# Last attention of a hybrid model: four exponentials per visit to the values, eight probability buffers, two buffers of masked keys, selections over 128 rows

## The reference

```
qkv = x @ W_qkv.T + b_qkv
scores = jnp.einsum('bqhd,bkhd->bhqk', Q, K)
scores = jnp.where(causal, scores, -jnp.inf)
probs = jax.nn.softmax(scores / sqrt(hd), axis=-1)
out = jnp.einsum('bkhd,bhqk->bqhd', V, probs)
return out @ W_o.T + b_o
```

## Time and profile before

| | us |
|---|---|
| median of 3 runs | 2612.34 |
| lowest, highest | 2611.93, 2614.21 |
| profiled execution | 2613.99 |
| its span, first to last instruction | 2612.3 |

### The profile page before, as it was taken

The page is one execution under the profiler, slowest core; times in us unless marked ns, Lnnn a source line. Parts: engine busy times, 40 slices in busy tenths (PEclk is TensorE's granted clock), DMA queues, the critical chain, the costliest instruction groups (busy, mean ns, idle before and its releaser), DMA issues. The chain is left out here.

```text
span 2612.3 us, 39415 instructions
## 1 busy us (share of the span) xinstructions
PE 2200.8 (84%) x12850; PEld 1667.5 (64%) x12850; DVE 1804.5 (69%) x5506; ACT 967.5 (37%) x1477; POOL 521.4 (20%) x526
## 2 busy tenths in 40 slices
PE   3777589988799987677667997799989999997999
PEld 2555479876688864545556986455555555556888
DVE  4778678863277867987877886666666666646787
ACT  1223034431144431111103443255656565563443
POOL 0000010100010102322311001244343344421000
PEclk8878689996689996666658998799999999997999
DMA  2000010000000000000000000000000000000000
GB/s 83 3 3 3 2 43 0 0 1 0 0 1 1 1 34 1 1 0 0 0 0 1 0 0 1 1 1 1 1 1 1 1 1 1 1 1 5 9 9 13
DMA packets 13993, 14.90 MB, mean 6 GB/s; under 512 B 3924, under 2 KB 11669, under 8 KB 13334
## 3 DMA queue, kind: packets, MB, share of 16 engines
q1 hardware_dynamic: 13846, 13.11, 1.6%
HBM read 10.22 MB, written 2.88 MB: 5 GB/s over the span
## 5 line engine op out<-in xcount | busy, mean ns | idle before, releaser
L2095 DVE TENSOR_REDUCE soft_mx<-psum 128x1 f32<-128x512 f32 (+3 forms) x608 | 381.0, 659 | 226.5 <-PE psum L1973 132.5
L2016 ACT ACTIVATE soft_prob<-psum 128x1024 f32<-128x1024 f32 (+3 forms) x384 | 306.4, 813 | 217.7 <-PE psum L1904 214.7
L1969 PE MATMUL psum<-soft_own,soft_stack 128*128 128x512 f32 (+3 forms) x768 | 248.3, 384 | 26.8 <-DVE soft_mx L2095 24.4
L1904 PE MATMUL psum<-soft_stack,soft_own 128*128 128x512 f32 (+3 forms) x768 | 233.2, 387 | 1.1 <-ACT soft_prob L2016 0.7
L1904 PEld LDWEIGHTS psum<-soft_stack,soft_own 128*128 128x128 f32 x768 | 119.9, 191 | 142.0 <-issue 89.2
L1969 PEld LDWEIGHTS psum<-soft_own,soft_stack 128*128 128x128 f32 x768 | 142.6, 196 | 80.0 <-DVE soft_mx L2095 62.3
L1919 PE MATMUL psum<-soft_prob,soft_v_pad 128*32 128x512 f32 (+3 forms) x1536 | 164.5, 500 | 5.2 <-ACT soft_prob L2016 3.3
L982 DVE SCALAR_TENSOR_TENSOR x<-psum,ffn1b_cw,x 128x128 f32 (+1 forms) x512 | 144.1, 344 | 32.1 <-PE psum L869 23.1
L982 DVE SCALAR_TENSOR_TENSOR x<-psum,ffn1a_cw,x 128x128 f32 (+1 forms) x512 | 144.1, 344 | 32.0 <-PE psum L869 22.8
L982 DVE SCALAR_TENSOR_TENSOR x<-psum,ffn0b_cw,x 128x128 f32 (+1 forms) x512 | 144.1, 344 | 31.8 <-PE psum L869 22.8
L982 DVE SCALAR_TENSOR_TENSOR x<-psum,ffn0a_cw,x 128x128 f32 (+1 forms) x512 | 144.1, 344 | 31.5 <-PE psum L869 22.5
(11 more groups left out here) (440 smaller groups left out, 4367.8 us busy)
## 6 DMA issues: line engine op xcount, KB each, us to landing
s_ffn_w<-in_ffn_w SPq DMA_DIRECT2D x4, 1024.0 KB, 6.0
out_x<-x SPq DMA_DIRECT2D x8, 256.0 KB, 2.3
mamba_coef_dram<-mamba_out_coef SPq DMA_DIRECT2D x8, 96.0 KB, 1.6
s_ret_w<-in_ret_w SPq DMA_DIRECT2D x1, 640.0 KB
s_ret_cos<-in_ret_cos SPq DMA_DIRECT2D x1, 512.0 KB
s_ret_sin<-in_ret_sin SPq DMA_DIRECT2D x1, 512.0 KB
s_mamba_in<-in_mamba_in SPq DMA_DIRECT2D x1, 256.0 KB
s_soft_sel<-in_soft_sel SPq DMA_DIRECT2D x1, 256.0 KB
```

The source lines that it names most:

```text
L1904: ins = pe.matmul(e_ps[:, n % 2, j, low(n):BLK], own[:, u % 3, 2 * pair + j, kt * P:(kt + 1) * P], stack[:, u % HT, qb * BLK + low(n):(qb ...
L1969: ins = pe.matmul(per_head[:, n, :], stack[:, u % HT, i * P:(i + 1) * P], own[:, u % 3, g, half * BLK:half * BLK + width], start=(n == 0), ...
L2016: nc.scalar.activation(prob[:, done % PROBS, :, low(n):BLK], e_ps[:, n % 2, :, low(n):BLK], ACT.Exp, scale=float(HD) ** -0.5).then_inc(exp ...
L2095: nc.vector.tensor_reduce(mx[:, i, half, heads.start:heads.stop], bank[:, 0:width * len(heads)].rearrange("p (g k) -> p g k", k=width), AX ...
```

## The change

- `PV_GROUP` = 4: PE visits the values at every fourth step, behind that step's scores, with two groups of eight matmuls, for the four exponentials before it. `prob` has eight buffers.
- `own` has two buffers, and `ao` one. `("own", u + 2, 0)` moves to step 23 of unit `u`, `("own", u + 2, 1)` to step 1 of unit `u + 1`, behind the other events there; POOL waits until all scores of the unit that used the buffer are issued.
- The maxima of the next unit begin at step 3 (`M_START`) and are spread over the 21 steps left.
- The selections `st` read all 128 partitions: `sel` exists once for each `t`, with the other rows zero (four scaled ACT copies). The causal mask is kept once and read once per head by a broadcast.

```diff
-PROBS = 4
+PROBS = 8
-PV_LAG = 4
+PV_GROUP = 4
+M_START = 3
...
             for j in range(M_JOBS):
-                at[j * E_STEPS // M_JOBS].append(("m", u + 1, j))
+                at[M_START + j * (E_STEPS - M_START) // M_JOBS].append(("m", u + 1, j))
         put((1, ("sh", u, 1)))
...
+        if 0 < u < UNITS - 1:
+            put((1, ("own", u + 1, 1)))
         if u + 2 < UNITS:
-            put((9, ("own", u + 2, 0)), (16, ("own", u + 2, 1)))
+            put((E_STEPS - 1, ("own", u + 2, 0)))
...
-        sel = sb("sel", [P, 2, 2, P], F32R)
+        sel = sb("sel", [P, HT, 2, 2, P], F32R)
-        causal = sb("causal_heads", [P, HT, P], F32R)
+        causal = sb("causal", [P, P], F32R)
-        own = sb("own", [P, 3, HT, SEQ], F32R)
+        own = sb("own", [P, 2, HT, SEQ], F32R)
-        ao = sb("ao", [P, 2, TPB, HEADS, HD])
+        ao = sb("ao", [P, TPB, HEADS, HD])
...
-                        if u >= 3:
-                            pool.wait_ge(score_ready, E_STEPS * (u - 2))
+                        if u >= 2:
+                            pool.wait_ge(score_ready, E_STEPS * (u - 1))
                         own_rows(nc.gpsimd, u, p, own_ready)
...
             def step(u, n):
-                if n % 2 == 0 and n >= PV_LAG:
-                    values(u, (n - PV_LAG) // 2)
-                elif n % 2 == 0 and u > 0:
-                    values(u - 1, PV_STEPS + (n - PV_LAG) // 2)
                 scores(u, n)
+                if n % PV_GROUP == 0 and (u or n):
+                    first = (E_STEPS * u + n - PV_GROUP) // 2
+                    for t in range(first, first + PV_GROUP // 2):
+                        values(*divmod(t, PV_STEPS))
...
-                    rows = slice(32 * t, 32 * t + 32)
                     pe.wait_ge(low_ready, 2 * (BPB * b + p) + i + 1)
                     for part in range(2):
-                        ins = pe.matmul(misc_ps[:, :, :], sel[rows, i, part, :], parts[rows, i, part, p * BLK:(p + 1) * BLK],
+                        ins = pe.matmul(misc_ps[:, :, :], sel[:, t, i, part, :], parts[:, i, part, p * BLK:(p + 1) * BLK],
...
-                        ins = pe.matmul(per_head[:, :, width - P:width], ident[:, :], causal[:, 0:len(heads), :],
+                        ins = pe.matmul(per_head[:, :, width - P:width], ident[:, :],
+                                        causal[:, :].unsqueeze(1).to_broadcast([P, len(heads), P]),
...
-            nc.scalar.copy(causal[:, :, :], w["causal"][:, :].unsqueeze(1).to_broadcast([P, HT, P]))
-            nc.scalar.copy(sel[:, :, :, :], w["sel"][:, :, :, :]).then_inc(sel_ready, 1)
+            nc.scalar.copy(causal[:, :], w["causal"][:, :])
+            for t in range(HT):
+                ins = nc.scalar.activation(sel[:, t, :, :, :], w["sel"][:, :, :, :], ACT.Copy, scale=w["head_rows"][:, t:t + 1])
+            ins.then_inc(sel_ready, 1)
```

More of the change, by code:

```diff
@@ L1824, in own_rows @@
             four = [P, HT, BLK]
-            eng.tensor_tensor(own[:, u % 3, :, now], keys[:, u % 2, now].unsqueeze(1).to_broadcast(four),
+            eng.tensor_tensor(own[:, u % 2, :, now], keys[:, u % 2, now].unsqueeze(1).to_broadcast(four),
                               w["head_rows"][:, :].unsqueeze(2).to_broadcast(four), ALU.mult).then_inc(done, 1)
@@ L1903, in scores @@
                 for j in range(2):
-                    ins = pe.matmul(e_ps[:, n % 2, j, low(n):BLK], own[:, u % 3, 2 * pair + j, kt * P:(kt + 1) * P],
+                    ins = pe.matmul(e_ps[:, n % 2, j, low(n):BLK], own[:, u % 2, 2 * pair + j, kt * P:(kt + 1) * P],
                                     stack[:, u % HT, qb * BLK + low(n):(qb + 1) * BLK], start=True, stop=True)
@@ L1969, in event @@
                         ins = pe.matmul(per_head[:, n, :], stack[:, u % HT, i * P:(i + 1) * P],
-                                        own[:, u % 3, g, half * BLK:half * BLK + width],
+                                        own[:, u % 2, g, half * BLK:half * BLK + width],
                                         start=(n == 0), stop=half != i // GT)
                     if half == i // GT:
-                        ins = pe.matmul(per_head[:, :, width - P:width], ident[:, :], causal[:, 0:len(heads), :],
+                        ins = pe.matmul(per_head[:, :, width - P:width], ident[:, :],
+                                        causal[:, :].unsqueeze(1).to_broadcast([P, len(heads), P]),
                                         start=False, stop=True)
@@ L1990, in event @@
                     for j in range(GT):
-                        ins = pe.transpose(misc_ps[:, j, :], ao[:, b % 2, GT * p + j, :, :], const["ident"][:, :])
+                        ins = pe.transpose(misc_ps[:, j, :], ao[:, GT * p + j, :, :], const["ident"][:, :])
                     ins.then_inc(misc_ready, 1)
@@ L1998, in _ @@
             run(event, step)
-            values(UNITS - 1, PV_STEPS - 2)
-            values(UNITS - 1, PV_STEPS - 1)
+            for t in range(PV_STEPS - PV_GROUP // 2, PV_STEPS):
+                values(UNITS - 1, t)
             for ev in END:
@@ L2118, in event @@
                     dve.wait_ge(rsum_ready, 2 * u + qb + 1)
-                    nc.vector.tensor_tensor(ao[:, b % 2, GT * qb:GT * (qb + 1), HT * t:HT * (t + 1), :], heads[:, :, :, 0:HD],
+                    nc.vector.tensor_tensor(ao[:, GT * qb:GT * (qb + 1), HT * t:HT * (t + 1), :], heads[:, :, :, 0:HD],
                                             wide(rsum[:, :, :], HD), ALU.mult).then_inc(misc_used, 1)
```

## The result

The changed kernel takes 2702.31 us (median of 4 runs, 2694.44 to 2708.16); the kernel before, beside it on the same chip, 2613.28. The ratio is 1.0339, with a 95% interval of 1.0309 to 1.0369: slower by 89 us where 36 were forecast, and outside the forecast's range (2608 to 2675). The profiled execution took 2694.44 us, its span is 2692.7.

What follows compares the result with a forecast made beforehand. The prediction took PE's instruction order to bound the kernel, with slack on POOL. Its sums by unit, 7.8 + 3.0 + 6.9 + 15.3 + 7.7 - 4.5 = +36 us on 2612.34, gave 2648 us, range 2608 to 2675.

Steps and rivals of the forecast that it cites:

- what the second buffer of masked keys costs: Visit of step 4, units 1 to 14: PE waits for masks queued behind POOL's second product, 2.8 us behind per unit.
- Rival one: Step 4 of each unit: POOL's queue is hidden after all, only the savings are left, 2575 us; chance 15%.
- the cancelling case: The queue gates, but late maxima are caught up beside other work and the clock stays: 2617 us; chance 16%.
- the wait for masks: Second half of the visit of step 4: PE stands idle 3 to 4 us until POOL's masks are done.
- the pace of the late maxima: Maxima 2 to 9, bunched between two visits, go at the pace of DVE's reductions through two banks; unit 4.1 us behind.
- The clock: After PE's new wait, 3.4 us at half clock cost 1.2 us in each of units 1 to 14, 17 us in all.
- fewer visits to the values: PE's visits per unit fall from twelve to six, 0.31 us saved each: 1.86 us a unit, 29.8 us over 16 units.
- selections of 128 rows: Selections over all 128 rows save PE 0.4 us per event at 56 events in units, bound 23 us.
- The worse case: Bunched maxima make DVE the pace between all visits, 2 us more per unit, 2675 us; chance 12%.

Runs made afterwards that it cites:

- own2: The kernel before with two buffers of masked keys alone (products at step 23 and next unit's step 1, maxima from step 3): 2700.38 us, ratio 1.0354.
- group4: The kernel before with visits to the values at every fourth step alone (six probability buffers, three key buffers): 2618.6 us, ratio 1.0023.
- own_behind_neg: The changed kernel with POOL's first product of masked keys waiting until DVE has negated the unit's maxima: 2709.93 us, ratio 1.0384.
- sel128_own_step12: The kernel before with 128-row selections and the second product of masked keys moved from step 16 to step 12: 2592.17 us, ratio 0.9929.
- sel128_own_12_16: The kernel before with 128-row selections and the second product at step 12, but at step 16 in units of t = 1: 2599.28 us, ratio 0.9952.

## Why the prediction was right in its sign and wrong in its size

**Right: what bounds the change.** The step "what the second buffer of masked keys costs" named the place, the queue and the wait. POOL's order is as written, PE waits for masks in the second half of the visit of step 4, and one digit that lets masks 2 and 3 pass takes 44 us away. The label alone misleads: own2 has the same queue and no wait for it, so the wait belongs to the visits of four as much as to the second buffer. Rival one (the queue is hidden) and the cancelling case are out.

**Right by size, with another filling: the loss of 92 us.** The forecast of +36 was the loss less 30 for visits and 23 for selections, so it put the loss at about 89. own2 measured 92. That the two agree is luck. The forecast filled the 89 with the wait for masks, the pace of the late maxima and the clock; own2 waits 0.5 us for masks and 45.3 for the negated maxima, a wait that the forecast had at nothing. In the changed kernel undoing the masks' queue takes 44 us away and, after that, undoing the wait for DVE 11; the start of the maxima at step 3, put alone into the kernel before, costs 34, a part of it again by DVE beside a product. These are differences in three different kernels, each with another share of half clock in it, and not shares of one sum.

**Wrong: "fewer visits to the values", 29.8 us.** This is the term that failed, 36 of the 53 us by which the forecast missed: grouping alone cost 6 us. Its price on PE was right: the visit of 512 and 384 columns at 1825.59 takes 1.64 us in one block, where two take 0.99 + 0.78 by the earlier trace rows and the second pays its entry and first weights again, and units 13 and 14 of group4 are shorter by 2.1 and 1.6 us. What failed is that PE's gain was taken for the kernel's in all 16 units. The runs show two costs that the term had at nothing. A visit of four takes its second pair of exponentials two steps sooner than the old order did: in units of t = 1 PE waits 3.27 us for mask 3 behind the norm's work, and these units lose 9.6 us. And a visit is now 1.6 to 1.9 us in which ACT gets no new scores, with two PSUM buffers in hand: the earlier trace rows carried the warning, ACT waits 15.7 us in unit 2 for PE's scores. In unit 15, where there are no maxima, PE waits for ACT too, so an exponential delayed comes back on PE; the prediction gave -0.5 there, measured was +3.0. Why units of t = 2, 3 and 0 keep only 0.2 to 0.3 of the 1.86 us stays open.

**Wrong by half: "selections of 128 rows", 23 us.** Measured 12, so 11 more of the 53. The saving per event is in the timeline in full; the units return a part as waiting. The rule of the Trainium skill that the prediction set against this part ("TensorE: Matmul & The Clock Gate", "Why this matters for your kernels": a matmul of 32 rows takes as long as one of 128) did not decide: by it alone nothing would have been gained.

**Missing: DVE beside POOL's product.** The change moved a POOL product of 3.6 us next to DVE's small instructions and the prediction priced only POOL's own queue. Rows that showed the effect stood in the trace of before, ahead of unit 0: the very instruction, 0.17 us in its 15 other places, takes 2.08 us beside a product.

```profile
1683.65 2.08 DVE L2105 TENSOR_TENSOR soft_mx<-soft_mx 128x16 f32<-128x16 f32 x1
```

```profile
1682.10 3.60 POOL L1825 TENSOR_TENSOR soft_own<-soft_keys,s_soft_head_rows 128x2048 fp32r<-128x2048 f32 x1 [5.90 <-ACT soft_keys L2038]
```

It ends at 1685.73, with the product (1685.70). In the changed kernel this instruction or the negation behind it takes 3.0 to 3.5 us in 11 of the 14 units concerned, all but units 2, 6 and 10, in which the product begins after them.

**The clock: the price fair, the places wrong.** The prediction put one stretch of 3.4 us at half clock into each of the units 1 to 14, at 1.2 us, 17 us in all. From first to last exponential the granted clock is 0.99 in the kernel before, 0.91 in own_behind_neg, and 0.95 in the changed kernel:

```profile
1677.70:2430.90 753.20, 635.11 (x3872) 404.43 (x3870) 444.85 (x806) 385.35 (x538) 269.81 (x339) 0.95 0.00 1
```

By the clock records of the traces that is 17 us at half clock before and 78 in the changed kernel: 18 stretches more. None lies in units 2, 6 and 10, one in each of t = 3 and t = 0, four in each of t = 1 (one or two before). So not all 14 units pay, and those of t = 1 pay more than once. Where units with the same list differ by a stretch (t = 1 in the kernel before, in sel128_own_step12 and in sel128_own_12_16), one costs 0.9 to 1.5 us, close to the 1.2 of the prediction. At that price the 18 are 16 to 27 us, an estimate from other kernels. It may be too high here: own_behind_neg has 51 us more at half clock than the changed kernel and is 8 to 12 us slower, with DVE's waits gone at the same time. No run takes the clock away alone, so its share isn't shown.

**The worse case** among the rivals, in which bunched maxima pace all visits, was the nearest in number. It was put at 2675 and given 12%. No run tests its mechanism; the 42.7 and 32.3 us that PE waits in the changed kernel are for masks and for the stretched DVE instructions, which it did not name.

## What to carry to other kernels

A saving on the engine that looks bound is worth only what its neighbours can take in the new rhythm. Grouping work moves it closer to what it needs: look for the youngest input of each group and at what stands ahead of it in its engine's queue (here mask 3, 3.27 us). And if the consumers hold two buffers, a long block on the producer can leave them without work (here ACT, 1.88 us), whatever it saves per entry. When a buffer is dropped, write down the queue of the engine that refills it from the moment the buffer comes free; what stands behind it there decided half of this change, together with the grouping. And before a long POOL instruction is moved, list the DVE instructions between SBUF and SBUF that will run beside it. Last, a total that agrees says little: own2 met the forecast's 89 us by waits that the forecast did not have.

## What the runs showed of the hardware

While a POOL product of 3.60 us that reads and writes SBUF runs, a DVE instruction of 16 elements from SBUF to SBUF stands until it ends: 3.27 us in place of 0.17; with the product moved by 1.1 us it takes 0.17 again. DVE reductions that read PSUM are not stretched: 45 of 512 columns that lie wholly beside products in the kernel before take 0.68 us (at most 0.69), the others 0.69. The Trainium skill has this rule: "SBUF — State Buffer", section "Terms", describes a port pair for which DVE and GpSimd hold an exclusive lock for the full instruction, the loser blocking fully. The runs agree, and they add a price: PE waits 32.3 us for it in the changed kernel and 45.3 in own2, and 11 us of time came back for 11 such places in the kernel without the masks' queue.

Selections over 32 partitions between matmuls over 128 cost 0.4 us a pair in spacing (0.46 against 0.86 us with their neighbours); over 128 partitions nothing.

A stretch of 3.4 us at a granted clock of 0.50, in a unit of t = 1 whose list of work is the same, goes with 0.9 to 1.5 us more time: units 5 and 9 of sel128_own_12_16 are alike to 0.03 us until the clock falls in one of them, and end 4.0 us apart with 3.4 and 13.7 us at half clock.
